# The tail of a fused four-layer kernel: another way to the final norm's reciprocal root, and the norm's scale and bias folded into other steps

## Chip, cores and metric

The kernel runs on one core of one Trainium2 chip, in one launch. The metric is the device time of that core in microseconds (us), taken as the median of several runs. All times below are from the runs and the profile of the kernel before.

## The reference, cut to what matters

Four layers follow one another on an input of 16 images of 48 channels and 16x16 pixels: a windowed attention network of six blocks, a sedenion mixer, an involution-like convolution and a gated scan in four directions (SS2D). Only the end of the last layer is touched. Its scan yields `y`, 8 images x 96 channels x 16 x 16, and then:

```
def layernorm2d(x, w, b, eps=1e-05):          # over the 96 channels of a pixel
    mu = x.mean(axis=1, keepdims=True)
    var = ((x - mu) ** 2).mean(axis=1, keepdims=True)
    return (x - mu) / jnp.sqrt(var + eps) * w[None, :, None, None] + b[None, :, None, None]

def grn(x, gamma, beta, eps=1e-06):           # over the 256 pixels of a channel
    Gx = jnp.sqrt(jnp.sum(x * x, axis=(2, 3), keepdims=True))
    Nx = Gx / (Gx.mean(axis=1, keepdims=True) + eps)
    return gamma[None, :, None, None] * (x * Nx) + beta[None, :, None, None] + x

y = jnp.einsum('bdchw,d->bchw', out_y, w_m)
y = layernorm2d(y, ln_w, ln_b)
y = grn(y, grn_gamma, grn_beta)
return conv1x1(y, W_out)                      # 96 channels -> 48
```

## The kernel before, in words

The program is written by hand for five engines. Each engine has one list of instructions that it runs in order, and semaphores tie the lists together. TensorE (PE) multiplies, VectorE (DVE) and ScalarE (ACT) work on the results, GpSimd (POOL) takes powers and issues accumulating DMAs, and SyncE (SP) issues loads and stores.

The last layer's scan is `unit(u)`, eight units: `u // 4` is the half batch `hb`, `u % 4` the direction. A unit's recurrence is 7 steps of 10 dependent instructions on DVE (L989 to L1001), on the tiles `gate`, `hst` and `prod`. After unit 7, DVE adds the last direction into `ysum[1]` (L1017); `ysum[0]` was finished four units before.

Then comes `tail(hb, stages)`, one function on each of PE, DVE and ACT. Each engine calls it stage by stage, and in each stage first for half 0 and then for half 1. A half is a tile of 128 partitions x 1536: the partitions are 4 groups (two images each) of 32 channels, and the 1536 columns are `G` = 3 channel groups of 512 pixels. The PSUM banks are `TAIL_BANK[hb]` and the one behind it: the program calls them `narrow` and `last` for half 0 and `scores_a` for both of half 1. `l3w` holds the layer's small weights, `Q_ONE` in it a block matrix of ones (the sum over a group's 32 lanes on every lane), `Q_IND` the same with one column per group. The stages are, for each half:

- **Mean.** PE multiplies the three 512-column groups by ones (L1797, six instructions, since an f32 product is issued as two). DVE subtracts the mean in three instructions (L1028), ACT squares in three (L1304), into `yqs[hb]`.
- **Variance.** PE uses the squares as weights against `Q_IND`: 12 products of four columns, 24 instructions (L1805), which leave pixels on partitions, 16 columns. DVE scales and adds eps (L1031) into `tvars`, POOL takes the power -0.5 (`tail_rstd`, L468), PE transposes (L1810), DVE copies into `rTs` (L1034), and PE spreads the result over all 128 partitions with the matrix `spread` (L1814, eight instructions).
- **Normalise.** DVE multiplies the three groups by it (L1039), into `yqs[hb]`.
- **Scale, bias, squares.** ACT applies the norm's scale and bias (L1309, three Identity instructions, `ysum[hb]`) and then squares with a sum along the row, six instructions of 256 pixels each followed by a read of the accumulator (L1315).
- **GRN factor.** POOL takes the root (`tail_norms`, L472), PE sums over channels (L1819, six instructions of two columns), DVE works out the factor in five small dependent instructions (L1045 to L1049) and applies it in six of 256 pixels (L1053), which write `yqs[hb]` in image order.
- **Output.** PE multiplies by `W_out` (L1826, twelve instructions a half in two sums of six), ACT copies each sum out of PSUM (L1322) into `ob[hb]`, SP stores it (L335).

The order of PE's list matters: the GRN sums of both halves (L1819) stand ahead of the output products of either (L1826). `step(op)` on DVE makes the next instruction wait for `op` by the semaphore `dve_step`. ScalarE's function table is set by hand once, ahead of the last layer (`preload_act_table_set`, just before L1282's loop): the set that holds Ln and Exp. `first_guess(u)` (L1249, L1252) takes Ln and Exp in every unit.

Of the kernel before, what the change touches and what calls it, by code (L numbers as in the profile page):

```python
# [60 lines left out]
M_MEAN, M_VAR, M_RT, M_SPREAD, M_GM, M_OUT, M_ALL = (int(n) for n in np.cumsum([0, 1, 1, 1, 1, 1, 2]))  # L61

A_YQ, A_NORM, A_SUM, A_OUT = 0, 3, 6, 12


D_YC, D_VAR, D_RT, D_YN, D_V2, D_ALL = (int(n) for n in np.cumsum([0, 3, 1, 1, 3, 6]))
# [14 lines left out]
def build(nc, x_tok, wpack, rpb_raw, mask_in, ident_in, ident2_in, en_in, fn_in,  # L81
          conv_in, sed_in, sign_in, l1_in, l2_in,
          front_in, taps_in, gates_in, l3_in, spread_in, out):
    with ExitStack() as ctx:
# [119 lines left out]
        tvars = [sb(f"tvar{i}", [128, 2, 16]) for i in range(2)]  # L204
        rTs = [sb(f"rT{i}", [16, 128]) for i in range(2)]
        gxs = [sb(f"gx{i}", [128, 6, 8]) for i in range(2)]
        yq = sb("yq", [128, HB])
# [5 lines left out]
        ob = [t[0:64 + C, 0:1024].rearrange("p (q k) -> p q k", q=2) for t in (ysum[0], guess)]  # L213
# [126 lines left out]
        def _(pool):  # L340
# [125 lines left out]
            def tail_rstd(hb):  # L466
                pool.wait_ge(tail_dve[hb], D_VAR + 1)
                pool.tensor_tensor(tvars[hb][:, 1], tvars[hb][:, 0], neg_half8[:], ALU.pow).then_inc(tail_pool[hb], 1)  # L468

# [30 lines left out]
            for hb in range(2):  # L500
                tail_rstd(hb)
# [4 lines left out]
        def _(dve):  # L506
# [512 lines left out]
            def tail(hb, stages):  # L1019
# [9 lines left out]
                if 1 in stages:  # L1029
                    dve.wait_ge(tail_pe[hb], M_VAR + 1)  # L1030
                    dve.tensor_scalar(tvars[hb][:, 0], B8[TAIL_BANK[hb]][:, 0:16], 1.0 / DIN, EPS, ALU.mult, ALU.add).then_inc(tail_dve[hb], 1)  # L1031
                if 2 in stages:
                    dve.wait_ge(tail_pe[hb], M_RT + 1)
                    dve.tensor_copy(rTs[hb][:], B8[TAIL_BANK[hb] + 1][0:16, 0:128]).then_inc(tail_dve[hb], 1)  # L1034
                if 3 in stages:
                    dve.wait_ge(tail_pe[hb], M_SPREAD + 1)
                    for g in range(G):
                        cols = slice(512 * g, 512 * (g + 1))
                        dve.tensor_tensor(yqs[hb][:, cols], B8[TAIL_BANK[hb]][:], yc[:, cols], ALU.mult).then_inc(tail_dve[hb], 1)  # L1039
                if 4 in stages:  # L1040
# [7 lines left out]
                    step(dve.tensor_tensor(per_group(2), per_group(4), l3w[:, Q_GRN:Q_GRN + G].unsqueeze(2).to_broadcast([128, G, 2]), ALU.mult))  # L1048
                    step(dve.tensor_scalar(gxs[hb][:, 5, 0:6], gxs[hb][:, 2, 0:6], 1.0, None, ALU.add))  # L1049
                    for g in range(G):  # L1050
                        for b in range(2):
                            j = 2 * g + b
                            dve.tensor_scalar(yqs[hb][:, 256 * j:256 * (j + 1)].rearrange("p (y x) -> p y x", x=16),  # L1053
                                              yc[:, 512 * g:512 * (g + 1)].rearrange("p (x y b) -> p b y x", y=16, b=2)[:, b],
                                              gxs[hb][:, 5, j:j + 1], l3w[:, Q_GRN + G + g:Q_GRN + G + g + 1], ALU.mult, ALU.add).then_inc(tail_dve[hb], 1)

            for c in range(4):
                middle_px(c)
            for u in range(8):
                unit(u)  # L1060
            for stage in range(5):
                tail(0, (stage,))
                tail(1, (stage,))

        @block.scalar
        def _(act):
# [231 lines left out]
            def tail(hb, stages):  # L1298
# [6 lines left out]
                if 1 in stages:  # L1305
                    for g in range(G):
                        cols = slice(512 * g, 512 * (g + 1))
                        act.wait_ge(tail_dve[hb], D_YN + g + 1)
                        act.activation(yc[:, cols], yqs[hb][:, cols], ACT.Identity, scale=l3w[:, Q_LN + g:Q_LN + g + 1],  # L1309
                                       bias=l3w[:, Q_LN + G + g:Q_LN + G + g + 1]).then_inc(tail_act[hb], 1)  # L1310
                    for g in range(G):
                        act.wait_ge(tail_act[hb], A_NORM + g + 1)
                        for b in range(2):
                            j = 2 * g + b
                            act.activation(yqs[hb][:, 256 * j:256 * (j + 1)], yc[:, 512 * g:512 * (g + 1)].rearrange("p (q b) -> p b q", b=2)[:, b],  # L1315
                                           ACT.Square, accum_out=gxs[hb][:, 0, j:j + 1]).then_inc(tail_act[hb], 1)
                if 2 in stages:
                    if hb == 0:
                        act.wait_ge(tail_dve[hb], D_V2 + 6)
# [19 lines left out]
            for stage in range(3):  # L1339
                tail(0, (stage,))  # L1340
                tail(1, (stage,))

        @block.tensor
        def _(pe):
# [439 lines left out]
            def tail(hb, stages):  # L1784
# [14 lines left out]
                if 1 in stages:  # L1799
                    for g in range(G):  # L1800
                        pe.wait_ge(tail_act[hb], A_YQ + g + 1)
                    for t in range(4):
                        for g in range(G):
                            first = 512 * g + 128 * t
                            op = pe.matmul(B8[TAIL_BANK[hb]][:, 4 * t:4 * t + 4], yqs[hb][:, first:first + 128], l3w[:, Q_IND:Q_IND + 4],  # L1805
                                           start=(g == 0), stop=(g == G - 1))
                    op.then_inc(tail_pe[hb], 1)
                if 2 in stages:
                    pe.wait_ge(tail_pool[hb], 1)
                    pe.transpose(B8[TAIL_BANK[hb] + 1][0:16, 0:128], tvars[hb][:, 1, :], ident[:]).then_inc(tail_pe[hb], 1)  # L1810
                if 3 in stages:
                    pe.wait_ge(tail_dve[hb], D_RT + 1)
# [271 lines left out]
```

## Time and profile before

| | us |
|---|---|
| median of 3 runs | 979.84 |
| lowest and highest | 979.49, 980.69 |
| the profiled execution, its own time | 981.16 |
| its span in the profile | 979.3 |

The span begins with the first instruction and ends with the last store; some 1.9 us of the profiled execution's time lie around it. In the profile PE is the matmul side of TensorE and PEld its weight loads. Engines' times of start are counted from the span's start. A line is one of the listing above, and a group joins instructions of one line, operation and tile. PEclk is the clock that TensorE was granted, 1.00 being 2.4 GHz and 0.50 being 1.2 GHz. "Idle before" is the time that the engine stood still ahead of an instruction, with what ended that.

### The profile page before, as it was taken

How to read it: one execution, taken by the hardware profiler on the slowest of the kernel's cores; microseconds unless marked ns; L12 is line 12 of the kernel's file. 1: busy time of each engine (PE TensorE's matmuls, PEld its weight loads, DVE VectorE, ACT ScalarE, POOL GpSimd, SP SyncE). 2: the span in 40 equal slices, each digit the busy share in tenths (PEclk: the TensorE clock that was granted, in tenths of full speed). 3: DMA queues.
4: the chain of work that ended last, by engine and by line, in shares of the span. 5: the costliest groups of instructions: out<-in, count | busy, mean ns of one | idle time of the engine just before them, and what ended most of it. 6: DMA issues, size and time to landing. Idle time of an engine off the chain costs nothing.

```text
span 979.3 us, 20396 instructions
## 1 busy us (share of the span) xinstructions
PE 801.5 (82%) x7980; PEld 534.8 (55%) x7980; DVE 794.5 (81%) x2001; ACT 574.2 (59%) x859; POOL 237.1 (24%) x272
## 2 busy tenths in 40 slices
PE   3799999999999999999999988799577668332366
PEld 1577877877787777777777764374211111000053
DVE  8788889988888998888899965755539999899942
ACT  1276777777777777777676663224466664645032
POOL 6122222222222222222222211382201221222021
PEclk8699999999999999999999997889676655565657
DMA  8200000000000000002000000100003665666301
GB/s 229 63 1 3 1 2 2 2 2 2 2 2 2 2 2 1 2 1 105 1 3 2 2 2 1 48 1 1 1 1 66 129 130 102 124 130 129 65 0 33
DMA packets 11621, 34.13 MB, mean 35 GB/s; under 512 B 1879, under 2 KB 4359, under 8 KB 11271
## 3 DMA queue, kind: packets, MB, share of 16 engines
q0 software_dynamic: 5904, 21.24, 11.5%
q1 hardware_dynamic: 5623, 11.60, 4.0%
q8 instruction: 64, 1.05, 0.4%
q14 instruction: 30, 0.25, 0.1%
HBM read 10.81 MB, written 0.79 MB: 12 GB/s over the span
## 4 chain that ended last, share of the span: by engine, by line
PE 62%; DVE 27%; ACT 5%; issue 3%; POOL 1%; DMA 1%; POOLq 0%; SPq 0%; DVEq 0%; ACTq 0%
PE narrow L1450 5%; PE wide L1373 4%; PE scores_a L1422 4%; PE scores_b L1422 4%; DVE prod L989 4%; PE last L1527 4%; DVE prod L997 3%; PE scores_a L1409 3%; PE scores_b L1433 3%; PE scores_b L1409 3%; PE scores_a L1433 3%; PE narrow L1480 3%; PE last L1523 2%; PE wide L1513 2%; PE last L1500 2%
## 5 line engine op out<-in xcount | busy, mean ns | idle before, releaser
L380 POOL TENSOR_TENSOR stb<-stb,neg_half 128x4 f32<-128x4 f32 x48 | 48.4, 1008 | 253.3 <-DVE stb L681 253.3
L1102 ACT ACTIVATE d<-d 128x768 f32<-128x768 f32 x96 | 80.6, 840 | 18.4 <-DVE d L628 17.9
L1450 PEld LDWEIGHTS narrow<-v,pt 128*64 128x64 f32 x2304 | 79.5, 139 | 13.4 <-issue 13.4
L1450 PE MATMUL narrow<-v,pt 128*64 128x54 f32 x2304 | 85.8, 225 | 0.1
L1697 PE MATMUL scores_b<-xb,gates_w 128*32 128x512 bf16 x192 | 26.0, 557 | 60.1 <-DVE yo L1009 51.4
L375 POOL TENSOR_TENSOR sta<-sta,neg_half 128x4 f32<-128x4 f32 x48 | 48.9, 1018 | 104.9 <-DVE sta L568 104.9
L1109 ACT ACTIVATE pt<-scores_a 128x768 f32<-128x768 f32 x48 | 38.9, 810 | 56.7 <-PE scores_a L1433 56.7
L1118 ACT ACT_TABLE_LOAD x47 | 60.3, 1283 | 0.8
L615 DVE TENSOR_REDUCE mx<-scores_a 128x12 f32<-128x768 f32 x48 | 46.0, 958 | 16.8 <-PE scores_a L1422 16.8
L1102 ACT ACT_TABLE_LOAD x46 | 59.0, 1283 | 0.8
L1118 ACT ACTIVATE ga<-wide 128x512 f32<-128x512 f32 x48 | 28.7, 598 | 49.6 <-PE wide L1513 49.5
L609 DVE COPY v<-narrow 64x96 f32<-64x96 f32 x192 | 48.9, 255 | 8.6 <-PE narrow L1385 6.6
L1527 PE MATMUL last<-wts,ga 128*128 128x48 f32 x384 | 55.5, 268 | 0.0
L628 DVE TENSOR_TENSOR d<-scores_a,mx 128x384 f32<-128x384 f32 x96 | 52.9, 552 | 1.7
L1373 PE MATMUL wide<-xa,wts 113*120 113x256 f32 x192 | 53.1, 401 | 0.8 <-ACT xa L1078 0.8
L1527 PEld LDWEIGHTS last<-wts,ga 128*128 128x128 f32 x384 | 51.5, 195 | 0.0
L475 POOL DMA_DIRECT2D gsum<-mag x28 | 26.0, 933 | 102.2 <-ACT gate L1239 67.9
L628 DVE TENSOR_TENSOR d<-scores_b,mx 128x384 f32<-128x384 f32 x96 | 49.1, 553 | 1.7
L1697 PEld LDWEIGHTS scores_b<-xb,gates_w 128*32 128x32 bf16 x192 | 5.0, 104 | 80.6 <-DVE yo L1009 55.3
L596 DVE TENSOR_TENSOR k<-wide,fn_gb 120x768 f32<-120x768 f32 x48 | 46.0, 958 | 2.7 <-PE wide L1373 1.3
L615 DVE TENSOR_REDUCE mx<-scores_b 128x12 f32<-128x768 f32 x48 | 45.7, 953 | 1.1 <-PE scores_b L1422 0.4
L989 DVE TENSOR_TENSOR prod<-gate,hst 128x288 f32<-128x288 f32 x112 | 45.8, 449 | 0.3
(351 smaller groups left out, 2200.9 us busy)
## 6 DMA issues: line engine op xcount, KB each, us to landing
gsum<-mag POOLq DMA_DIRECT2D x14, 512.0 KB, 4.6
ysum<-yo POOLq DMA_DIRECT2D x7, 768.0 KB, 5.8
ysum<-xd POOLq DMA_DIRECT2D x6, 768.0 KB, 5.8
gsum<-mag POOLq DMA_DIRECT2D x14, 256.0 KB, 4.7
wts<-in_wpack SPq DMA_DIRECT2D x6, 442.0 KB, 6.7
sed_w<-in_sed_in SPq DMA_DIRECT2D x1, 2304.0 KB, 8.0
graw<-in_gates_in SPq DMA_DIRECT2D x1, 1152.0 KB, 5.1
x_all<-in_x_tok SPq DMA_DIRECT2D x8, 96.0 KB, 3.2
```

The lines of the kernel that those rows point to most:

```text
L375: pool.tensor_tensor(st[n % 2].sta[:, 1], st[n % 2].sta[:, 0], neg_half[:, 0:TILES], ALU.pow).then_inc(rstd1, 1)
L615: dve.tensor_reduce(st[n % 2].mx[:, u], sc_bank[u][:, :, 0:SC].rearrange("p r (g m) -> p r g m", m=N), AX.X, ALU.max).then_inc(mx_ready[u], 1)
L628: dve.tensor_tensor(t.d[:, u::2, 3 * r:3 * r + 3, :], s, mx, ALU.subtract).then_inc(d_ready[u], 1)
L989: dve.tensor_tensor(prod[:, n], gates, neighbours(x - 1), ALU.mult).then_inc(dve_step, 1)
L1102: act.activation(d, d, ACT.Exp).then_inc(p_ready[u], 1)
L1118: act.activation(t.g1[:], hid_bank[:, :, 0:256], ACT.Gelu).then_inc(g1_made, 1)
L1373: op = pe.matmul(hid_bank[0:120, part, 0:256], w[0:WIN, col:col + 120], t.xa[0:WIN, :], start=True, stop=True)
L1409: pe.matmul(dst, ident2[:], rhs, start=(part == 0), stop=(part == 1))
L1422: op = pe.matmul(sc_bank[u][64 * b:64 * b + 64, r, 192 * v:192 * v + 192], t.q[rows, cols], t.k[rows, :, cols], start=False, stop=True, sk ...
L1433: op = pe.transpose(sc_bank[u][:, v, 128 * h:128 * (h + 1)], t.d[:, 2 * v + u, 2 * h:2 * h + 2].rearrange("p h m -> p (h m)"), ident[:])
L1450: op = pe.matmul(y_ps[64 * b:64 * b + 64, q * VO:(q + 1) * VO], t.pt[:, q, h, 64 * b:64 * b + 64], t.v[:, q, b, h * VO:(h + 1) * VO], star ...
L1527: op = pe.matmul(z_ps[:, col:col + C], t.g1[:, u, 128 * b:128 * b + 128], w[:, W_2A:W_2A + C], start=False, stop=True, skip_group_check=True)
```

## The change

The variance is now summed by products with the block of ones, so that it comes out on all 128 partitions at once, into the bank behind the mean's. ACT takes Ln and Exp of it (a guess of the reciprocal root), and DVE makes one Newton step of three instructions on 512 columns. The power on POOL, the transpose, the copy and the spreading product are gone. The norm's scale and bias go into the squares' own scale and bias on ACT, and into the factors of DVE's last scaling, by products prepared once in a small tile `fold`. The output products read `ysum[hb]` now, and the copies out go to `yqs[hb]`. For both halves, not for half 0 alone, ACT waits for the last scaling ahead of the copies.

```diff
-        tvars = [sb(f"tvar{i}", [128, 2, 16]) for i in range(2)]
-        rTs = [sb(f"rT{i}", [16, 128]) for i in range(2)]
         gxs = [sb(f"gx{i}", [128, 6, 8]) for i in range(2)]
+        fold = sb("fold", [128, 10])
...
-        ob = [t[0:64 + C, 0:1024].rearrange("p (q k) -> p q k", q=2) for t in (ysum[0], guess)]
+        ob = [t[0:64 + C, 0:1024].rearrange("p (q k) -> p q k", q=2) for t in yqs]
...
-            def tail_rstd(hb):
-                pool.wait_ge(tail_dve[hb], D_VAR + 1)
-                pool.tensor_tensor(tvars[hb][:, 1], tvars[hb][:, 0], neg_half8[:], ALU.pow).then_inc(tail_pool[hb], 1)
...
-            for hb in range(2):
-                tail_rstd(hb)
...
                 if 1 in stages:
-                    dve.wait_ge(tail_pe[hb], M_VAR + 1)
-                    dve.tensor_scalar(tvars[hb][:, 0], B8[TAIL_BANK[hb]][:, 0:16], 1.0 / DIN, EPS, ALU.mult, ALU.add).then_inc(tail_dve[hb], 1)
-                if 2 in stages:
-                    dve.wait_ge(tail_pe[hb], M_RT + 1)
-                    dve.tensor_copy(rTs[hb][:], B8[TAIL_BANK[hb] + 1][0:16, 0:128]).then_inc(tail_dve[hb], 1)
-                if 3 in stages:
-                    dve.wait_ge(tail_pe[hb], M_SPREAD + 1)
+                    r, t = mag[hb][:, 0:512], mag[hb][:, 512:1024]
+                    dve.wait_ge(tail_act[hb], A_GUESS + 1)
+                    step(dve.scalar_tensor_tensor(t, B8[TAIL_BANK[hb] + 1][:], DIN * EPS, r, ALU.add, ALU.mult))
+                    step(dve.scalar_tensor_tensor(t, t, -0.5 / DIN, r, ALU.mult, ALU.mult))
+                    step(dve.scalar_tensor_tensor(t, t, 1.5, r, ALU.add, ALU.mult))
                     for g in range(G):
                         cols = slice(512 * g, 512 * (g + 1))
-                        dve.tensor_tensor(yqs[hb][:, cols], B8[TAIL_BANK[hb]][:], yc[:, cols], ALU.mult).then_inc(tail_dve[hb], 1)
-                if 4 in stages:
+                        dve.tensor_tensor(yqs[hb][:, cols], t, yc[:, cols], ALU.mult).then_inc(tail_dve[hb], 1)
+                if 2 in stages:
...
-                    step(dve.tensor_tensor(per_group(2), per_group(4), l3w[:, Q_GRN:Q_GRN + G].unsqueeze(2).to_broadcast([128, G, 2]), ALU.mult))
-                    step(dve.tensor_scalar(gxs[hb][:, 5, 0:6], gxs[hb][:, 2, 0:6], 1.0, None, ALU.add))
+                    for k, col in ((2, 0), (5, G)):
+                        op = dve.tensor_tensor(per_group(k), per_group(4), fold[:, col:col + G].unsqueeze(2).to_broadcast([128, G, 2]), ALU.mult)
+                        chain[0] += 1
+                        op.then_inc(dve_step, 1)
+                    dve.wait_ge(dve_step, chain[0])
+                    for k, add in ((2, l3w[:, Q_LN:Q_LN + G]), (5, fold[:, 2 * G:3 * G])):
+                        op = dve.tensor_tensor(per_group(k), per_group(k), add.unsqueeze(2).to_broadcast([128, G, 2]), ALU.add)
+                        chain[0] += 1
+                        op.then_inc(dve_step, 1)
+                    dve.wait_ge(dve_step, chain[0])
...
-                            dve.tensor_scalar(yqs[hb][:, 256 * j:256 * (j + 1)].rearrange("p (y x) -> p y x", x=16),
-                                              yc[:, 512 * g:512 * (g + 1)].rearrange("p (x y b) -> p b y x", y=16, b=2)[:, b],
-                                              gxs[hb][:, 5, j:j + 1], l3w[:, Q_GRN + G + g:Q_GRN + G + g + 1], ALU.mult, ALU.add).then_inc(tail_dve[hb], 1)
+                            dve.tensor_scalar(yc[:, 256 * j:256 * (j + 1)].rearrange("p (y x) -> p y x", x=16),
+                                              yqs[hb][:, 512 * g:512 * (g + 1)].rearrange("p (x y b) -> p b y x", y=16, b=2)[:, b],
+                                              gxs[hb][:, 2, j:j + 1], gxs[hb][:, 5, j:j + 1], ALU.mult, ALU.add).then_inc(tail_dve[hb], 1)
+            step(dve.memset(fold[:, 9:10], EPS))
+            gamma, ln_w, ln_b = l3w[:, Q_GRN:Q_GRN + G], l3w[:, Q_LN:Q_LN + G], l3w[:, Q_LN + G:Q_LN + 2 * G]
+            for op in (dve.tensor_tensor(fold[:, 0:G], gamma, ln_w, ALU.mult), dve.tensor_tensor(fold[:, G:2 * G], gamma, ln_b, ALU.mult),
+                       dve.tensor_tensor(fold[:, 2 * G:3 * G], l3w[:, Q_GRN + G:Q_GRN + 2 * G], ln_b, ALU.add)):
+                chain[0] += 1
+                op.then_inc(dve_step, 1)
+            dve.wait_ge(dve_step, chain[0])
             for c in range(4):
                 middle_px(c)
...
                 if 1 in stages:
+                    r = mag[hb][:, 0:512]
+                    act.wait_ge(tail_pe[hb], M_VAR + 1)
+                    act.activation(r, B8[TAIL_BANK[hb] + 1][:], ACT.Ln, scale=1.0 / DIN, bias=fold[:, 9:10]).then_inc(tail_act[hb], 1)
+                    act.wait_ge(tail_act[hb], A_LN + 1)
+                    act.activation(r, r, ACT.Exp, scale=-0.5).then_inc(tail_act[hb], 1)
+                if 2 in stages:
...
-                        act.activation(yc[:, cols], yqs[hb][:, cols], ACT.Identity, scale=l3w[:, Q_LN + g:Q_LN + g + 1],
-                                       bias=l3w[:, Q_LN + G + g:Q_LN + G + g + 1]).then_inc(tail_act[hb], 1)
-                    for g in range(G):
-                        act.wait_ge(tail_act[hb], A_NORM + g + 1)
                         for b in range(2):
                             j = 2 * g + b
-                            act.activation(yqs[hb][:, 256 * j:256 * (j + 1)], yc[:, 512 * g:512 * (g + 1)].rearrange("p (q b) -> p b q", b=2)[:, b],
-                                           ACT.Square, accum_out=gxs[hb][:, 0, j:j + 1]).then_inc(tail_act[hb], 1)
-                if 2 in stages:
-                    if hb == 0:
-                        act.wait_ge(tail_dve[hb], D_V2 + 6)
+                            act.activation(yc[:, 512 * g + 256 * b:512 * g + 256 * b + 256], yqs[hb][:, cols].rearrange("p (q b) -> p b q", b=2)[:, b],
+                                           ACT.Square, scale=l3w[:, Q_LN + g:Q_LN + g + 1], bias=l3w[:, Q_LN + G + g:Q_LN + G + g + 1],
+                                           accum_out=gxs[hb][:, 0, j:j + 1]).then_inc(tail_act[hb], 1)
+                if 3 in stages:
+                    act.wait_ge(tail_dve[hb], D_V2 + 6)
...
                 if 1 in stages:
                     for g in range(G):
                         pe.wait_ge(tail_act[hb], A_YQ + g + 1)
-                    for t in range(4):
-                        for g in range(G):
-                            first = 512 * g + 128 * t
-                            op = pe.matmul(B8[TAIL_BANK[hb]][:, 4 * t:4 * t + 4], yqs[hb][:, first:first + 128], l3w[:, Q_IND:Q_IND + 4],
-                                           start=(g == 0), stop=(g == G - 1))
+                        op = pe.matmul(B8[TAIL_BANK[hb] + 1][:], ones, yqs[hb][:, 512 * g:512 * (g + 1)], start=(g == 0), stop=(g == G - 1))
                     op.then_inc(tail_pe[hb], 1)
                 if 2 in stages:
                     pe.wait_ge(tail_pool[hb], 1)
-                    pe.transpose(B8[TAIL_BANK[hb] + 1][0:16, 0:128], tvars[hb][:, 1, :], ident[:]).then_inc(tail_pe[hb], 1)
-                if 3 in stages:
-                    pe.wait_ge(tail_dve[hb], D_RT + 1)
-                    for t in range(4):
-                        op = pe.matmul(B8[TAIL_BANK[hb]][:, 128 * t:128 * (t + 1)], spread[:, t, :], rTs[hb][:], start=True, stop=True)
-                    op.then_inc(tail_pe[hb], 1)
...
-                            op = pe.matmul(B8[TAIL_BANK[hb] + q][0:112, :], l3w[:, col:col + 112], yqs[hb][:, 512 * g:512 * (g + 1)],
+                            op = pe.matmul(B8[TAIL_BANK[hb] + q][0:112, :], l3w[:, col:col + 112], ysum[hb][:, 512 * g:512 * (g + 1)],
```

## Rows read from the trace of the kernel before

**Rows 1.** Busy time, share of the span and instructions of each engine:

```profile
PE 801.5 (82%) x7980; PEld 534.8 (55%) x7980; DVE 794.5 (81%) x2001; ACT 574.2 (59%) x859; POOL 237.1 (24%) x272
```

**Rows 2.** Chain that ended last, 931 us to the end: start, duration, what

```profile
931.24 5.46 PE scores_a L1797 x6
...
939.54 4.16 PE scores_a L1805 x24
...
943.97 2.91 POOL tvar L468
...
949.35 0.70 DVE yq L1039
...
950.07 2.22 ACT ysum L1309 x3
952.30 2.49 ACT yq L1315 x12
...
962.38 5.30 PE narrow L1826 x6
```

**Rows 3.** Timeline, 939 us to the end: start, duration, instructions, idle before them

```profile
939.58 0.17 DVE L1031 TENSOR_SCALAR tvar<-narrow 128x16 f32<-128x16 f32 x1 [0.95 <-PE narrow L1805]
...
954.68 2.21 ACT L1309 ACTIVATE ysum<-gate,l3w 128x512 f32<-128x512 f32 x3
...
957.70 0.16 DVE L1045 TENSOR_SCALAR gx<-last 128x2 f32<-128x2 f32 x1 [4.68 <-PE last L1819]
...
958.71 2.54 DVE L1053 TENSOR_SCALAR yq<-ysum,gx,l3w 128x256 f32<-128x256 f32 x6
...
959.18 0.19 ACT L1315 ACTIVATION_READ_ACCUMULATOR gate<-ysum 128x1 f32 x1
959.45 1.44 POOL L472 TENSOR_TENSOR gx<-gx,half 128x6 f32<-128x6 f32 x1 [3.27 <-ACT gate L1315]
960.94 1.35 PEld L1819 LDWEIGHTS scores_a<-gx,l3w 128*128 128x128 f32 x6 [3.36 <-POOL gx L472]
...
962.24 5.44 PE L1826 MATMUL narrow<-yq,l3w 128*112 128x512 f32 x6
...
970.24 5.31 PE L1826 MATMUL scores_a<-gate,l3w 128*112 128x512 f32 x12
```

**Rows 4.** Stretches of the tail: bounds, length, busy time (instructions), then granted clock

```profile
931.00:937.00 6.00, 5.76 (x10) 2.69 (x10) 3.36 (x7) 1.82 (x3) 0.00 (x0) 0.50 0.00 0
937.00:940.00 3.00, 3.00 (x28) 3.00 (x28) 1.80 (x4) 1.83 (x3) 0.10 (x1) 0.98 0.00 0
...
941.00:962.00 21.00, 9.50 (x42) 8.59 (x43) 7.79 (x20) 9.29 (x30) 7.50 (x4) 0.50 0.00 0
962.00:967.00 5.00, 5.00 (x8) 2.21 (x9) 3.37 (x11) 0.00 (x0) 0.00 (x0) 0.50 0.01 3
...
968.00:976.00 8.00, 7.55 (x18) 2.83 (x16) 0.00 (x0) 1.98 (x4) 0.00 (x0) 1.00 0.28 74
```

**Rows 5.** Groups by line, 930 us to the end: busy us, mean ns, idle before

```profile
L1309 ACT ACTIVATE ysum<-gate,l3w 128x512 f32<-128x512 f32 x3 | 2.2, 799 | 0.0
...
L1028 DVE SCALAR_TENSOR_TENSOR ysum<-scores_a,ysum 128x512 f32<-128x512 f32 x3 | 1.9, 685 | 2.6 <-PE scores_a L1797 2.6
...
L1304 ACT ACTIVATE gate<-ysum 128x512 f32<-128x512 f32 x3 | 1.8, 630 | 2.7 <-DVE ysum L1028 2.7
```

**Rows 6.** Groups of ACT by line and shape, from 560 us on

```profile
L1249 ACT ACTIVATE guess<-gsum,gate_eps 128x512 f32<-128x512 f32 x8 | 5.8, 722 | 3.4 <-DMA gsum<-mag 2.0 <-DVE gsum L937 1.4
L1252 ACT ACTIVATE guess<-guess 128x512 f32<-128x512 f32 x8 | 4.9, 616 | 0.0
```

**Rows 7.** Timeline of ACT, the last load of a function table in the trace

```profile
694.10 1.28 ACT L1282 ACT_TABLE_LOAD   x1
```

**Rows 8.** Timeline of DVE ahead of the last layer's first instruction

```profile
722.50 1.28 DVE L925 CAST xb<-wide 32x512 bf16<-32x512 f32 x2 [19.80 <-PE wide L1764]
```

**Rows 9.** Groups of DVE by line and shape, 727 to 932 us, a scan instruction

```profile
L989 DVE TENSOR_TENSOR prod<-gate,hst 128x288 f32<-128x288 f32 x112 | 45.8, 449 | 0.3
```

More of the change, by code:

```diff
@@ L56 @@
 L2_COLS = U_BIAS + 1
-M_MEAN, M_VAR, M_RT, M_SPREAD, M_GM, M_OUT, M_ALL = (int(n) for n in np.cumsum([0, 1, 1, 1, 1, 1, 2]))
-A_YQ, A_NORM, A_SUM, A_OUT = 0, 3, 6, 12
-D_YC, D_VAR, D_RT, D_YN, D_V2, D_ALL = (int(n) for n in np.cumsum([0, 3, 1, 1, 3, 6]))
+M_MEAN, M_VAR, M_GM, M_OUT, M_ALL = (int(n) for n in np.cumsum([0, 1, 1, 1, 2]))
+A_YQ, A_LN, A_GUESS, A_SUM, A_OUT = 0, 3, 4, 5, 11
+D_YC, D_YN, D_V2, D_ALL = (int(n) for n in np.cumsum([0, 3, 3, 6]))
 X3_BANK = (3, 6, 7, 6, 7, 6)
@@ L1060, in _ @@
                 unit(u)
-            for stage in range(5):
+            for stage in range(3):
                 tail(0, (stage,))
@@ L1338, in _ @@
                 first_guess(u)
-            for stage in range(3):
+            for stage in range(4):
                 tail(0, (stage,))
@@ L1809, in tail @@
                     pe.wait_ge(tail_pool[hb], 1)
-                    pe.transpose(B8[TAIL_BANK[hb] + 1][0:16, 0:128], tvars[hb][:, 1, :], ident[:]).then_inc(tail_pe[hb], 1)
-                if 3 in stages:
-                    pe.wait_ge(tail_dve[hb], D_RT + 1)
-                    for t in range(4):
-                        op = pe.matmul(B8[TAIL_BANK[hb]][:, 128 * t:128 * (t + 1)], spread[:, t, :], rTs[hb][:], start=True, stop=True)
-                    op.then_inc(tail_pe[hb], 1)
-                if 4 in stages:
-                    pe.wait_ge(tail_pool[hb], 2)
                     for g in range(G):
@@ L1820, in tail @@
                     op.then_inc(tail_pe[hb], 1)
-                if 5 in stages:
+                if 3 in stages:
                     for q in range(2):
@@ L1851, in _ @@
                     gates(u + 2, (0,))
-            for stage in range(6):
+            for stage in range(4):
                 tail(0, (stage,))
```

## Prediction

> **What bounds the kernel now.** I read the page's busy times first: PE and DVE are each busy for about four fifths of the span [rows 1], so no engine is idle enough to make the whole kernel a one-engine question, and the changed part has to be read on its own. The chain that ended last shows it. From 931 us the chain goes back and forth between engines, in short pieces [rows 2]: mean products, variance products, the power on POOL, the normalising multiplication on DVE, then ACT without a break, and at the end the output products. So the tail (931.2 to 979.3 us, 48 us of the span) is a chain of latencies, and every us taken from it comes off the kernel's time. What bounds it can be read at three places of the timeline.
>
> First, the detour over POOL. Half 0's variance sums are complete when DVE starts at 939.58 [rows 3], and its normalising multiplication starts at 949.35 [rows 2]: 9.8 us, in which POOL takes 2.91 us for each half's power.
>
> Second, ACT. Scale and bias of half 0 start at 950.07 [rows 2], half 1's at 954.68, and half 1's last accumulator read ends at 959.18 + 0.19 = 959.37 [rows 3]. ACT works through all of it, 9.3 us for two halves, 2.2 us of Identity and 2.5 us of squares each.
>
> Third, the gate in PE's order. The output products of half 0 start only at 962.24, behind half 1's GRN sum, although half 0's scaling was through at 958.71 + 2.54 = 961.25 [rows 3]. So the end is set by half 1's last square: 959.37, then POOL 1.44 us, the GRN sum at 960.94, output products from 962.24 [rows 3], and 17 us of output products, copy and store after them, which the change leaves alone. I follow one number through the change: when the output products can start.
>
> **The change, step by step,** on the trace's own time axis.
>
> *Variance.* PE is free of the mean products at about 936.5, and half 0's squares are there by then. Six 512-column instructions take 5.44 us with drain at the low clock and twelve take 5.31 us at the high one [rows 3], less some 0.2 us of drain 0.87 and 0.43 us each. TensorE's clock was at 1.2 GHz up to 937 and at 2.4 GHz from shortly after [rows 4], after 5.9 us of gapless products that began at 931.24. With the rise at the same place the first instruction is mostly low and five are high: done at 936.5 + 0.75 + 5 x 0.43 = 939.4, with 0.16 us of drain 939.6. That is what the 24 small instructions reached as well (939.58), so half 0 gains nothing here. Half 1 follows at 939.4 + 6 x 0.43 = 942.0, drained 942.1, against 943.70 [rows 2].
>
> *Guess.* On ACT, Ln with a bias pointer 0.72 us and Exp 0.62 us [rows 6], with 0.03 us between them for the wait: half 0 at 939.6 + 1.4 = 941.0, half 1 at 942.1 + 1.4 = 943.5. The trace has no Ln from PSUM; bounds are 0.60 and 0.80 us, from rows 5's cheapest and dearest 512-column ACTIVATE, so 0.1 us either way.
>
> *Newton step and multiplication.* The nearest row for a 512-column scalar_tensor_tensor is 0.685 us [rows 5]. Dependent small DVE instructions come every 0.20 us where each takes 0.16 (five from 957.70 to 958.71 [rows 3]), so a wait adds some 0.03 us: three steps 2.15 us. The three multiplications go at 0.60 us intervals, the first ready 0.69 us after its start. Half 0: 943.1, first result 943.8, last 945.0. Half 1 waits for DVE, not for its guess (943.5): 945.0 to 947.1, first result 947.8, last 949.0.
>
> *Squares.* The three Identity instructions of a half are gone, 2.2 us each. In exchange the squares carry a scale and a bias pointer. Identity with both takes 0.799, Square with neither 0.630 [rows 5]: 0.17 us more each. Six pairs of square and accumulator read took 2.49 us [rows 2]; they now take 2.49 + 6 x 0.17 = 3.5. Half 0: 943.8 to 947.4. Half 1: 947.8 to 951.4. Here is the new bound of half 1: 959.37 becomes 951.4.
>
> *Behind it.* POOL's root, the GRN sum and PE's order are as before, 2.87 us from the last square to the first output product (959.37 to 962.24), so these start at 954.3. Half 0's scaling must be there too: squares end 947.4, GRN factor's first DVE instruction 3 us later (950.4, the same chain of POOL and PE), seven small DVE instructions in place of five, two pairs of them independent, 1.2 us; six scalings 2.54 us [rows 3]: 954.1, the last just in time, as PE needs it 1.7 us after its first. Half 1's are through by 958.3, and PE wants them at 962.1.
>
> *At nothing.* The three products and the memset for `fold` run on DVE, in 19.8 us of idle time ahead of L925 [rows 8]; without that cover they would cost 0.8 us. The wait that ACT now has for half 1's scaling (958.3) ends before the products that it copies. POOL loses 5.8 us of powers and has nothing queued behind them but the roots. No load and no store is added; SP's waits are the same two per half. The tiles behind `fold` lie 1,240 bytes lower than before (two `tvars` and two `rTs` gone, `fold` in). Nothing in the trace prices that. The scan's instructions on `prod` run 449 ns for the large ones [rows 9]; I take no change, and keep 0.5 us on either side.
>
> **The sum:** 962.24 - 954.3 = 7.9, or by half 1's last square 8.0. I take 8.0 us. On the profiled execution that is 979.3 to 971.3 of span (981.16 to 973.2); on the median, 979.84 - 8.0 = 971.8. The profiled execution is 1.3 us above the median, which is an offset and not part of the difference.
>
> **Rivals.**
>
> *The variance is summed at the low clock.* The small four-column products gave way to twelve full ones, and what they cost hangs on the clock. If it rises only behind them, half 0 is complete at 936.5 + 6 x 0.87 + 0.2 = 941.9 and half 1 at 947.1; the guess of half 1 is there at 948.5, its first product 2.8 us later at 951.3, the squares end at 954.9, and the gain is 4.5 us: 975.3. For it: the clock stood low through the whole mean. Against it: in this trace it rose at 937 with no more than such products before it. Chance 0.12.
>
> *The output products warm up earlier.* They started low and went high after 5.6 us or so [rows 4]. The new start lies elsewhere relative to whatever makes the clock rise. Three instructions fewer at the low clock save 3 x 0.43 = 1.3 us: 970.5. Chance 0.13.
>
> *Slower: TensorE stays low through the tail.* Between 941 and 962 it was at 1.2 GHz, in spite of 9.5 us of work [rows 4], and the new tail has other work and other pauses. Variance low costs 3.5 of the 8.0 us. Then 18 of the 24 output instructions, now high, would take 0.43 us more each, 7.7 us: 979.84 - 4.5 + 7.7 = 983.0. It decides from the point where 11 of these 18 stay low (4.5 / 0.43). Against it: both runs of gapless 512-column products in this trace brought the clock up. Chance 0.03.
>
> *Ln and Exp reload the function table,* so that the change doesn't do what it says. Then every change between them costs a load of 1.28 us [rows 7]. Four loads: half 0's guess at 943.6, half 1's at 947.6, DVE free at 947.6, squares end 954.0, gain 5.4: 974.4. Against it: 16 Ln and 16 Exp in the scan, and the last load is at 694 us [rows 6, 7]. The Trainium skill, "ScalarE: Activation LUTs", section "What ACT_TABLE_LOAD costs", speaks against such a switch more strongly: it adds a drain and comes to about 2.66 us for each. An estimate by that figure, with four switches, puts half 1's guess at 953.0 and the gain at nothing, 979.8. The same page's section on table sets names one set that holds both functions, and with that the trace agrees. Chance of either form 0.03.
>
> **Numbers.** Forecast 0.69, variance at the low clock 0.12, earlier rise 0.13, table loads 0.03, low throughout 0.03. About 0.2%, 2 us, is what can be told from no change here. All but the last two, and these in part, are faster by more: 0.94 faster, 0.03 the same, 0.03 slower. The range takes in the earlier rise with 0.5 us for the moved tiles, and the low variance with as much: 970.0 to 975.8.
>
> **What would show it.** In the profile after: Ln on ACT at about 939.6 and half 1's last accumulator read at about 951.4; each square 0.58 us instead of 0.41; the first output product near 954.3, 2.9 us behind the last square; no table load behind 694; scan steps unchanged. The forecast is wrong if variance products show a granted clock of 0.50, if a gap opens on DVE between the halves' Newton steps, or if the output products take longer than 13.3 us from first to last.

## The result, and the profile after

The changed kernel takes 970.56 us (median of 5 runs, 968.84 to 971.04) against 979.67 us before (median of 5, 976.84 to 980.69): a ratio of 0.9906 with a 95% interval of 0.9887 to 0.9925, that is by the ratio 9.2 us less, with an interval of 7.3 to 11.1. A second series of the same two kernels gave 969.94 us, again a ratio of 0.9906 (0.9882 to 0.993). Forecast were 971.8 us, 8.0 us less.

The chain that ended last in the changed kernel, from half 1's mean products on (start, duration, what), answers to [rows 2]:

```profile
930.00 5.46 PE scores_a L1805 x6
935.45 2.59 PE last L1810 x6
...
938.07 0.69 ACT mag L1314
...
938.79 0.64 ACT mag L1316
...
939.45 0.70 DVE mag L1025
...
941.63 0.70 DVE yq L1030
...
942.35 3.73 ACT ysum L1323 x12
...
952.94 4.16 PE narrow L1822 x6
```

POOL's power and the spreading products are gone from it, and ACT no longer has an Identity pass. Between the last piece of one engine and the first of the next there are two or three hundredths of a us. From half 0's first variance product to its first normalising multiplication it was 936.70 to 949.35 in the kernel before, 12.7 us, with half 1's variance products and power in between [rows 2]. It is 935.45 to 941.63 now, 6.2 us. The row of the kernel before with which this stretch begins:

```profile
936.70 2.84 PE narrow L1805 x24
```

The timeline of the changed kernel answers to [rows 3] (start, duration, instructions, idle before them):

```profile
940.64 0.69 ACT L1314 ACTIVATE mag<-scores_a,fold 128x512 f32<-128x512 f32 x1 [1.23 <-PE scores_a L1810]
...
943.44 0.69 DVE L1025 SCALAR_TENSOR_TENSOR mag<-scores_a,mag 128x512 f32<-128x512 f32 x1
...
945.61 1.90 DVE L1030 TENSOR_TENSOR gate<-mag,ysum 128x512 f32<-128x512 f32 x3
...
949.86 0.18 ACT L1323 ACTIVATION_READ_ACCUMULATOR ysum<-gate,l3w 128x1 f32 x1
...
950.12 1.32 POOL L467 TENSOR_TENSOR gx<-gx,half 128x6 f32<-128x6 f32 x1 [2.00 <-ACT ysum L1323]
...
952.80 4.29 PE L1822 MATMUL narrow<-ysum,l3w 128*112 128x512 f32 x6
...
959.51 5.31 PE L1822 MATMUL scores_a<-ysum,l3w 128*112 128x512 f32 x12
```

Two traces can't be subtracted by their time of start, since the tail begins 1.24 us earlier in this one. That is not the scan's doing: from the last layer's first CAST on DVE to half 1's mean it took 208.7 us before [rows 8] and takes 209.2 now (720.76 to 930.00). The lead is there ahead of the layer already. The measure that I use from here on is the time from half 1's first mean product to the first output product, *the chain* for short. It was 962.24 - 931.24 = 31.0 us and is 952.80 - 930.00 = 22.8 us: 8.2 us less. From the first output product to the end of the span it was 979.3 - 962.24 = 17.1 us and is 968.2 - 952.80 = 15.4 us: 1.7 us less, though only the tiles that this stretch reads and writes were changed, and one wait. 1.3 of it lie between the first output product and the end of ACT's last copy (976.19 before, 965.46 after), the rest in the last store. The windows say why for the greater part (bounds, length, busy time and count of PE, PEld, DVE, ACT, POOL, then PEclk):

```profile
930.00:932.00 2.00, 2.00 (x3) 0.96 (x4) 2.00 (x4) 0.31 (x1) 0.00 (x0) 0.50 0.00 0
...
937.00:940.00 3.00, 3.00 (x8) 1.33 (x7) 0.93 (x2) 2.36 (x4) 0.00 (x0) 1.00 0.00 0
...
950.00:958.00 8.00, 6.50 (x15) 3.54 (x16) 6.66 (x25) 0.64 (x2) 1.32 (x1) 0.64 0.00 0
958.00:966.00 8.00, 6.82 (x16) 2.48 (x14) 0.00 (x0) 1.79 (x3) 0.00 (x0) 1.00 0.26 74
```

The variance products ran at 2.4 GHz, as forecast. The output products began at 1.2 GHz in both, but the clock rose sooner: the first six took 4.29 us against 5.44 [rows 3].

New and changed instructions, grouped by line (busy us, mean ns, idle before):

```profile
L1323 ACT ACTIVATE ysum<-gate,l3w 128x256 f32<-128x256 f32 x6 | 3.6, 602 | 0.3 <-DVE gate L1030 0.3
...
L1316 ACT ACTIVATE mag<-mag 128x512 f32<-128x512 f32 x2 | 1.3, 630 | 0.1
...
L1314 ACT ACTIVATE mag<-last,fold 128x512 f32<-128x512 f32 x1 | 0.7, 687 | 0.0
```

### The profile page after: what moved, and what is told of

The parts are those of the page before. It is cut to its first block, busy times and chain, and to the rows that moved or that the text cites. A ratio compares the mean times of both kernels' runs of the same rounds, so it can differ in the third digit from the quotient of the medians.

```text
span 968.2 us, 20293 instructions
## 1 busy us (share of the span) xinstructions
PE 796.0 (82%) x7926; PEld 526.2 (54%) x7926; DVE 798.8 (83%) x2011; ACT 574.5 (59%) x857; POOL 231.4 (24%) x270
## 4 chain that ended last, share of the span: by engine, by line
PE 62%; DVE 27%; ACT 5%; issue 3%; DMA 1%; POOL 1%; POOLq 0%; SPq 0%; DVEq 0%; ACTq 0%
PE narrow L1458 6%; PE wide L1381 4%; PE scores_a L1430 4%; PE scores_b L1430 4%; DVE prod L982 4%; PE last L1535 4%; DVE prod L990 3%; PE scores_b L1441 3%; PE scores_a L1417 3%; PE scores_b L1417 3%; PE scores_a L1441 3%; PE narrow L1488 3%; PE last L1531 2%; PE wide L1521 2%; PE last L1508 2%
```

## Experiments

### The same kernel once more: what varies by itself

No edit.

> The changed kernel once more, unaltered, to see what differs between executions of one program. Theory: the chain from the first mean product of half 1 to the first output product is fixed (22.8 us in the profile after, against 31.0 before, a gain of 8.2), and what differs is where TensorE's clock rises: the first six output instructions took 4.3 us in that profile and 5.4 before. So here again 22.8 within 0.3 us for the chain, and between 4.2 and 5.4 us for those six, with total times that lie in clusters some 2 us apart. Rival: part of the 9 us of gain is in the scan ahead of the tail (moved tiles); then the first mean product comes 1 us or more earlier than before also in this profile.

```profile
928.45 4.78 PE L1805 MATMUL scores_a<-ysum,l3w 128*128 128x512 f32 x6 [15.57 <-DVE ysum L1010]
...
950.56 5.44 PE L1822 MATMUL narrow<-ysum,l3w 128*112 128x512 f32 x6
```

The chain took 22.1 us, not 22.8. That missed the bound of 0.3 us, and for one reason: the clock rose within the mean products this time (4.78 us for six, against 5.46), so the chain itself contains a clock that varies. The first six output products took 5.44 us here, as before the change. So the 1.15 us by which they were shorter in the profile after are not fixed by the change, and 0.7 us of the chain come and go. Total times were 968.54 to 971.28 us and one of 975.26, whose cause is open; the first series has two groups, 968.8 to 969.0 and 970.6 to 971.0, this one has no clear ones. The groups go with the clock: TensorE's mean granted clock was 0.881 and 0.883 in the faster two executions of the first series, 0.871 in the slower three. From 700 to 750 and from 750 to 800 us it was 0.69 and 0.68 in the profile after and 0.76 and 0.75 in this one, of the same program, and the tail began 1.55 us earlier here. So part of what differs lies ahead of the tail.

The rival named a sign, a first mean product 1 us or more earlier than before also in this profile, and the sign came true: 928.45 against 931.24. It came true for another reason than the scan, which took 208.6 to 209.2 us from the layer's first CAST to half 1's mean in all twelve profiles; its large instruction on `prod` takes 451 ns against 449 [rows 9]. The start of half 1's mean lay between 927.6 and 930.8 us in all ten later profiles, also at 929.46 in one of a kernel that is the one before up to the tail, so part of the lateness of 931.24 is chance. Another part may not be. Between 20 and 30 us, in code that no edit touches, TensorE's mean granted clock was 0.54 and 0.55 in the two profiles of kernels without the tile `fold`, and 1.00 in all ten with it, the kernel with the old variance path and `fold` among them. ACT's second load of a function table, long ahead of the first instruction that was edited, stands at 51.48 and 51.27 us in those two, and at 49.7 to 51.8 us in the ten, at 50.5 on average. Up to about 1 us of the measured gain may lie there. Whether the moved tiles bring it about was not tested.

### The variance path alone

The new variance and root, with Identity, squares, factor and output as before:

```diff
+                        act.activation(yc[:, cols], yqs[hb][:, cols], ACT.Identity, scale=l3w[:, Q_LN + g:Q_LN + g + 1],
+                                       bias=l3w[:, Q_LN + G + g:Q_LN + G + g + 1]).then_inc(tail_act[hb], 1)
...
+                            act.activation(yqs[hb][:, 256 * j:256 * (j + 1)], yc[:, 512 * g:512 * (g + 1)].rearrange("p (q b) -> p b q", b=2)[:, b],
+                                           ACT.Square, accum_out=gxs[hb][:, 0, j:j + 1]).then_inc(tail_act[hb], 1)
```

> The new variance and root alone: scale and bias are still applied by three Identity instructions a half, then squares, factor and output as before. Theory: the first normalised group of half 0 is there 12.3 us after the first mean product, as with the whole change (18.8 before), and from there ACT works 9.3 us without a break, to 21.6 us after that product against 28.1 before. So 6.5 of the 8.1 us. Rival, that the folded scale and bias carry the gain: less than 3 us here.

```profile
930.28 5.46 PE L1795 MATMUL scores_a<-ysum,l3w 128*128 128x512 f32 x6 [16.35 <-DVE ysum L1010]
...
942.88 2.22 ACT L1307 ACTIVATE ysum<-yq,l3w 128x512 f32<-128x512 f32 x3 [0.36 <-DVE yq L1030]
...
954.94 5.31 PE L1812 MATMUL narrow<-yq,l3w 128*112 128x512 f32 x6
```

ACT begins 12.6 us after the mean's start, and the chain is 24.66 us: 6.3 us less than before, 6.5 expected. The time was 973.24 us, ratio 0.9929 (0.9904 to 0.9954). The rival, that the folded scale and bias carry the gain, is out.

### Scale and bias folded alone

The old variance path, with the squares taking scale and bias, the factors from `fold`, and the output read from `ysum`:

```diff
-                        act.activation(yc[:, cols], yqs[hb][:, cols], ACT.Identity, scale=l3w[:, Q_LN + g:Q_LN + g + 1],
-                                       bias=l3w[:, Q_LN + G + g:Q_LN + G + g + 1]).then_inc(tail_act[hb], 1)
...
+                            act.activation(yc[:, 512 * g + 256 * b:512 * g + 256 * b + 256], yqs[hb][:, cols].rearrange("p (q b) -> p b q", b=2)[:, b],
+                                           ACT.Square, scale=l3w[:, Q_LN + g:Q_LN + g + 1], bias=l3w[:, Q_LN + G + g:Q_LN + G + g + 1],
```

> Scale and bias folded alone; variance by small products, power on POOL, transpose and spreading as before. Theory: ACT starts as before (18.8 us after the first mean product) and needs two times 3.7 us in place of two times 4.6, so half 1's last square ends 26.2 us after that product, against 28.1: 1.9 us gained. Rival, that the folded scale and bias carry the gain: 5 us or more.

```profile
930.03 5.46 PE L1808 MATMUL scores_a<-ysum,l3w 128*128 128x512 f32 x6 [16.36 <-DVE ysum L1018]
...
952.56 0.59 ACT L1326 ACTIVATE ysum<-gate,l3w 128x256 f32<-128x256 f32 x1
...
959.02 4.85 PE L1837 MATMUL narrow<-ysum,l3w 128*112 128x512 f32 x6
```

The chain is 28.99 us, 2.0 us less than before, 1.9 expected. Half 1's squares start 22.5 us after the mean's start, straight behind half 0's. The time was 977.18 us, ratio 0.998 (0.9966 to 0.9995). With 6.3 for the variance path the parts make 8.3 us, and the whole 8.2: they add. By the ratios they are 7.0 and 2.0 us against 9.2, which agrees, though each of the three has an interval of its own, of some 1.4 to 2.4 us on either side.

### Without the Newton step

The three instructions of each half are left out, so the factor is the guess by Ln and Exp alone:

```diff
-                    step(dve.scalar_tensor_tensor(t, B8[TAIL_BANK[hb] + 1][:], DIN * EPS, r, ALU.add, ALU.mult))
-                    step(dve.scalar_tensor_tensor(t, t, -0.5 / DIN, r, ALU.mult, ALU.mult))
-                    step(dve.scalar_tensor_tensor(t, t, 1.5, r, ALU.add, ALU.mult))
...
-                        dve.tensor_tensor(yqs[hb][:, cols], t, yc[:, cols], ALU.mult).then_inc(tail_dve[hb], 1)
+                        dve.tensor_tensor(yqs[hb][:, cols], r, yc[:, cols], ALU.mult).then_inc(tail_dve[hb], 1)
```

> The changed kernel without the Newton step: the three scalar_tensor_tensor of each half are left out, and the guess itself is the factor. Theory: they are on the path for half 0 (2.2 us), and then ACT's squares bind: half 0's squares run from 10.2 to 13.9 us after the first mean product, half 1's to 17.6, against 20.0 with the step. 2.5 us gained. If both halves' steps were on the path: 4.3 us. If ACT's work hid them: none.

```profile
930.06 4.86 PE L1802 MATMUL scores_a<-ysum,l3w 128*128 128x512 f32 x6 [15.50 <-DVE ysum L1010]
...
938.91 1.90 DVE L1027 TENSOR_TENSOR yq<-mag,ysum 128x512 f32<-128x512 f32 x3 [2.07 <-ACT mag L1313]
...
940.82 0.63 ACT L1313 ACTIVATE mag<-mag 128x512 f32<-128x512 f32 x1
...
941.36 0.60 ACT L1320 ACTIVATE ysum<-yq,l3w 128x256 f32<-128x256 f32 x1
...
951.54 4.34 PE L1819 MATMUL narrow<-ysum,l3w 128*112 128x512 f32 x6
```

The expectation failed. The chain is 21.5 us, 0.6 less than in the second profile of the changed kernel, whose mean took about as long, where 2.5 were expected. The rows show the reason. Half 0's first normalised group is there at 938.91 + 0.70 = 939.6, but its first square starts at 941.36, right behind half 1's Exp. In ACT's order Ln and Exp of half 1 stand ahead of half 0's squares, and they can't come earlier, since half 1's variance is not summed before 940.1. So most of the Newton step is covered by the wait for the other half's guess. I had put that Ln and Exp into ACT's schedule in the forecast and forgot it when I took the step away. The time was 969.95 us (ratio 0.9898, 0.9877 to 0.9919), no different from the changed kernel's.

### Two Newton steps

```diff
+                    w = mag[hb][:, 1024:1536]
+                    step(dve.scalar_tensor_tensor(w, B8[TAIL_BANK[hb] + 1][:], DIN * EPS, t, ALU.add, ALU.mult))
+                    step(dve.scalar_tensor_tensor(w, w, -0.5 / DIN, t, ALU.mult, ALU.mult))
+                    step(dve.scalar_tensor_tensor(t, w, 1.5, t, ALU.add, ALU.mult))
```

> The changed kernel with a second Newton step, three more scalar_tensor_tensor of 512 columns a half. Leaving the one step out brought 0.6 to 1.3 us on the way to the output products, where 2.5 was expected. Reading: without it, half 0's squares wait for half 1's Ln and Exp, which stand ahead of them in ACT's order and come no earlier. If that is right the step is nearly free only in that direction: a second one has no such cover, comes after both guesses, and is on DVE's path for both halves, 2 x 2.15 = 4.3 us. Rival, that DVE's steps are hidden behind something in general: under 1.5 us, as with the first.

```profile
927.79 4.70 PE L1809 MATMUL scores_a<-ysum,l3w 128*128 128x512 f32 x6 [15.65 <-DVE ysum L1010]
...
941.57 0.62 ACT L1327 ACTIVATE ysum<-yq,l3w 128x256 f32<-128x256 f32 x1 [2.54 <-DVE yq L1034]
...
947.01 1.90 DVE L1034 TENSOR_TENSOR gate<-mag,ysum 128x512 f32<-128x512 f32 x3
947.73 0.62 ACT L1327 ACTIVATE ysum<-gate,l3w 128x256 f32<-128x256 f32 x1 [2.44 <-DVE gate L1034]
...
954.23 5.12 PE L1826 MATMUL narrow<-ysum,l3w 128*112 128x512 f32 x6
```

The chain is 26.4 us against 22.1: 4.3 us more, as expected. ACT now waits for DVE ahead of both halves' squares, 2.54 and 2.44 us. The time was 976.06 us, ratio 0.9955 (0.9936 to 0.9974). That is 5.5 and 6.1 us above the changed kernel in its two series, more than the chain shows; the profile is of the fastest execution (972.6 us of 972.6 to 977.3), so what the others lost beyond the chain isn't shown. The same three instructions a half bring 0.6 us when the step is taken away and cost 4.3 when a second is added. With one step, DVE and ACT are near balance: DVE is a little behind ACT, and ACT's idle time ahead of the squares is 0.36 and 0.27 us.

### Keeping TensorE's clock up, with the change

Additional f32 products of 128x512 into a bank that nobody reads, in PE's idle time; all that the kernel computes stays in it. The diff has the numbers of the last of the four kernels:

```diff
+            def warm(n):
+                for _ in range(n):
+                    pe.matmul(B8[2][:], l3w[:, Q_ONE:Q_ONE + 128], x3[:, 0, 0:512], start=True, stop=True)
...
             for stage in range(4):
                 tail(0, (stage,))
+                if stage == 0:
+                    pe.wait_ge(gate_taken[2], 21)
+                warm((18, 0, 2, 0)[stage])
                 tail(1, (stage,))
+                warm((0, 9, 0, 0)[stage])
```

First with 8 behind the variance and 2 between the GRN sums, none ahead of the mean:

> The changed kernel with ten additional f32 products of 128x512 on TensorE into a bank that nobody reads: eight between the variance and the GRN sum of half 0, two between the GRN sums. They compute nothing that is used. Theory: TensorE has nothing to do there (7.5 us ahead of half 0's GRN sum), and the fillers keep its clock at 2.4 GHz, so all 24 output instructions take 0.43 us each: 10.5 us with drain, against 12.0 in the profile after and 13.4 in the one taken again. With faster GRN sums 2 to 3 us less in all. Rival, that the two short GRN stretches let the clock fall all the same: the first six output instructions still take 4.3 to 5.4 us, and the time is that of the changed kernel.

```profile
948.56 0.83 PE L1815 MATMUL last<-gx,l3w 128*128 128x2 f32 x6 [0.71 <-POOL gx L467]
...
952.67 2.81 PE L1822 MATMUL narrow<-ysum,l3w 128*112 128x512 f32 x6
```

```profile
950.00:955.00 5.00, 4.23 (x15) 1.95 (x14) 4.73 (x19) 0.44 (x2) 1.41 (x1) 1.00 0.00 0
```

The clock stays at 2.4 GHz through the GRN sums, each of which takes 0.83 us in place of 1.44, and the first six output products take 2.81 us. The time was 969.01 us (ratio 0.9891, 0.9873 to 0.9909), about 1 us below the changed kernel in its two series (970.56, 969.94), by medians of different series; 2 to 3 were expected. The spread shrank: 967.9 to 969.8.

Then with 15 ahead of the mean alone, and with both sets:

> The changed kernel with fifteen additional f32 products of 128x512 ahead of half 1's mean products, while the scan keeps DVE busy and TensorE idle (15 us). Theory: the mean's six instructions take 2.8 us in place of 4.8 to 5.5, half 1's squares end 2.0 to 2.6 us earlier, and with them Ln of half 0, which stands behind them in ACT's order. 2 to 2.6 us less. Rival: half 0's chain is bound by DVE's subtractions and not by the mean products; then less than 1 us. Other rival: the fillers run too long at the low clock and delay the mean.

> Both sets of fillers. If they are independent, the gains add: 4 to 5.5 us less than the changed kernel, some 965 us. If the mean's fillers already leave the clock high long enough, the second set brings less than alone.

Neither did what was meant. 970.95 us (ratio 0.9908, 0.9888 to 0.9929) for the first is no gain, and 968.74 (0.9888, 0.9869 to 0.9906) for both is the gain of the second set. The mean's rows, in the first kernel and in that with both, show the miss:

```profile
927.59 4.51 PE L1805 MATMUL scores_a<-ysum,l3w 128*128 128x512 f32 x6 [2.83 <-DVE ysum L1010]
```

```profile
930.17 5.46 PE L1805 MATMUL scores_a<-ysum,l3w 128*128 128x512 f32 x6 [3.71 <-DVE ysum L1010]
```

The fillers ended too early: PE stood still for 2.83 and 3.71 us, and the clock was down for most or all of the mean. So I closed that gap, with 18 ahead of the mean and 9 and 2 behind the variance:

> As with both sets of fillers, but eighteen ahead of half 1's mean products in place of fifteen, and nine in place of eight behind the variance. In the two runs with fifteen, TensorE stood idle for 2.8 and 3.7 us between the last filler and the mean, and the granted clock was down again when the mean began. Theory: with the gap closed, the mean's six instructions take 2.8 us in place of 5.5 (4.5 to 5.5 in all profiles up to here), and 2 to 2.6 us more come off than with the second set alone: some 966.5 us. Rival: half 1 gains nothing from an earlier mean because ACT's squares of both halves stand ahead of Ln; then the time stays at 968.7. Other rival: fillers overrun and delay the mean by up to 1 us.

```profile
930.83 2.81 PE L1805 MATMUL scores_a<-ysum,l3w 128*128 128x512 f32 x6 [1.11 <-DVE ysum L1010]
```

```profile
925.00:929.00 4.00, 4.00 (x10) 1.73 (x10) 3.97 (x19) 0.00 (x0) 0.00 (x0) 1.00 0.00 0
...
930.00:932.00 2.00, 1.17 (x3) 0.68 (x4) 2.00 (x5) 0.00 (x0) 0.00 (x0) 1.00 0.00 0
```

After 1.11 us of rest the clock is still up, and the mean takes 2.81 us. The first output product starts at 950.48, so the chain is 19.65 us. The time was 966.38 us (965.95 to 966.72), ratio 0.9858 (0.9835 to 0.988): the fastest version here, 12.6 us below the 979.02 that the kernel before took in the same series, against 9.2 for the change alone. It does more work than the changed kernel and is faster.

### Keeping the clock up, without the change

The kernel before, with 5 fillers behind the spreading products and 3 between the GRN sums:

```diff
+                warm((0, 0, 0, 0, 3, 0)[stage])
                 tail(1, (stage,))
+                warm((0, 0, 0, 5, 0, 0)[stage])
```

> The kernel before, with eight additional f32 products of 128x512 into a bank that nobody reads: five behind the spreading products, three between the two GRN sums. It separates the clock from the change. Theory: the clock is high when the output products start and in both GRN sums, so the products take 10.5 us in place of 13.3 and the tail 3 us less: some 977. Compared with the changed kernel that has such fillers (969.0), the change itself is then worth 8 us, as the chain to the first output product says. Rival: the change's gain is mostly a luckier clock; then this kernel comes within 3 us of 969.

```profile
929.46 4.80 PE L1797 MATMUL scores_a<-ysum,l3w 128*128 128x512 f32 x6 [15.56 <-DVE ysum L1017]
...
960.38 2.81 PE L1826 MATMUL narrow<-yq,l3w 128*112 128x512 f32 x6
```

976.94 us (976.43 to 977.78), ratio 0.9972 (0.9957 to 0.9986). With the output products at the same clock in both, old and new kernel stand at 976.94 and 969.01 us: 7.9 us apart. The chains of the two profiles are 30.9 and 22.3 us (929.46 to 960.38, 930.36 to 952.67), 8.6 apart. So a luckier clock in the output products is out as the main cause of the gain. The fillers don't flatter the comparison: in this kernel they held up half 0's GRN sum by 1.3 us, but half 1's, which gates the output, waited for POOL. The clock in half 1's variance products isn't evened out: it fell in their midst here (5.25 us for 24), and was at 2.4 GHz in the 512-column products that replace them (2.74 us for six in the profile after). That is a part of the change's gain.

## Why the prediction was right

The forecast's mechanism held at every step of the chain, and the total fell inside the range. Point by point, in us after half 1's first mean product, forecast (its time minus 931.24) and the profile after (its time minus 930.00):

| step | forecast | measured |
|---|---|---|
| half 0's variance complete, Ln starts | 8.4 | 8.07 |
| half 1's variance complete, Ln starts | 10.9 | 10.64 |
| half 0's guess ready, DVE takes it up | 9.8 | 9.45 |
| half 0's normalising multiplication starts | 11.9 | 11.63 |
| half 1's starts | 15.9 | 15.61 |
| half 1's last accumulator read ends | 20.2 | 20.04 |
| first output product | 23.1 | 22.80 |

Two small errors cancel in the last rows: everything up to the normalising multiplications was 0.2 to 0.3 us earlier than forecast, and each half's squares took 0.2 us longer. That the forecast of half 1's last read is only 0.1 us off is in this part luck.

- **Variance.** That half 0 would gain nothing from the larger products was nearly so: the clock rose a little sooner. Half 1's came 1.8 us sooner relative to the mean (it was 943.72 - 931.24 = 12.5). The rival with a low clock in the variance didn't occur in any profile with the new path: six products took 2.7 to 3.0 us in all of them, and in all of them the mean's products stand directly ahead.
- **Guess.** 0.69 and 0.63 us for Ln and Exp, against 0.72 and 0.62. Ln reads PSUM, and lies within its two bounds.
- **Newton step.** 0.69 us each, 0.72 from start to start, 2.18 for three: 2.15 forecast. That DVE and not the guess of half 1 would gate half 1 was right too (guess ready at 941.99, DVE free at 943.4).
- **Squares.** The added 0.17 us for the two pointers was 0.19: 602 to 608 ns against 414. 3.7 us a half, 3.5 forecast.
- **Order of PE.** Half 0's scaling was forecast to end 0.2 us ahead of the first output product. The six scalings end at 950.80 + 2.54 = 953.34, 0.54 us after it, since POOL's first root took 1.90 us, where the forecast had reckoned with the 1.32 of the kernel before. It cost nothing: the product that needs the last scaling is the fifth instruction, and PE's first six took no longer than their clock explains.
- **The 8.0 us.** The chain gives 8.2 in the profiles, the pair with fillers 7.9. The measured 9.2 (7.3 to 11.1) contains 8.0; the point forecast was short by 1.2 us. The part of it that a profile shows is the clock in the output products, 1.15 us, my second rival with its 1.3 us. But the second profile of the same kernel lacks it. Among the seven profiles with a new path or `fold` and without fillers ahead of the output, the six products took 4.29, 4.34, 4.85, 5.12, 5.31, 5.44 and 5.44 us. Whether their new place raises the chance of an earlier rise stays open, since the kernel before has one profile without fillers. The other candidate is the clock ahead of the tail, where the forecast had kept 0.5 us for moved tiles: up to about 1 us, as said above, with its cause open.
- **Table loads.** Ln and Exp cost none. The Trainium skill, "ScalarE: Activation LUTs", section on table sets, says that one set holds both, and the trace agrees: the last load on ACT in the profile after is still the one ahead of the layer. The 2.66 us that the Trainium skill gives on that page, under "What ACT_TABLE_LOAD costs", for a switch with its drain is not what the trace before shows: the load at 694.10 [rows 7] starts 0.02 us after the end of the ACTIVATE ahead of it, and the next ACTIVATE starts at 695.39, 1.3 us in all. So the 1.28 us by which the rival was priced was the right one of the two.

```profile
692.39 1.28 ACT L1288 ACT_TABLE_LOAD   x1
```

- **At nothing.** The setup of `fold` runs on DVE from 701.06 to 701.94 us, ahead of an idle stretch of 18.8 us, so it shows nowhere in the chain, and the scan's instructions are unchanged to 2 ns.

The slower rival, TensorE low through the tail, didn't occur. What was shown is the other end of it: held up throughout, the same kernel takes 966.4 us.

## What to carry to other kernels

At the end of a kernel, where engines work in turns, write the chain out with each engine's order and ask which of two halves a step gates; the same three instructions were worth 0.6 us less when taken away and 4.3 more when doubled. A detour over a slow engine costs its hand-overs too: 9.8 us went by between half 0's variance and its normalisation. POOL's two powers were 5.8 us of it, but the first ran beside half 1's variance products; in PE's order half 0's spreading products stood behind these and behind half 1's transpose, which waited for the second power, and so half 0 waited for half 1. And where short bursts of products alternate with waiting, idle TensorE time may be spent on products that nobody reads, if they last until the next burst.

## What the runs showed that I had not expected

- Six 512-column f32 products took 5.46, 4.86, 4.80, 4.78, 4.70, 4.51 or 2.81 us at the same place in the program, by where the clock rose. A chain that starts with TensorE at rest carries 0.7 us of chance for each such burst, and compared profiles have to be read with it in mind.
- Fillers that ended 3.7 us before the burst did nothing for it, those that ended 1.1 us before it saved 2.65 us on six products. With 2.8 us in between the six took 4.51 us, little less than the 4.70 to 4.86 that four profiles without such fillers show.
- The first root on POOL after some 33 us of rest took 1.90 us and the second 1.32 in the changed kernel (1.32 and 1.44 before, where powers had run shortly before). It lay off the path, though the chain's listing leads through it: the second root waited for ACT's last square. The run without the Newton step had 1.35 after 32.4 us of rest and that with two 1.35 after 33.8, so rest alone doesn't explain it, and the cause is open.
